# Spreading the reciprocals of the denominators through device memory instead of with matmuls

## The chip, the core and the metric

The kernel runs on one core of one Trainium2 chip. The metric is the device time of one execution in microseconds (us). Before the change the median of three runs is 1918.21 us (1917.11 to 1920.19).

## The reference, cut to what matters

The input is 16 sequences of 1024 tokens with 512 features (16384 tokens). The attention layer is a causal linear attention with 16 heads of 32 features, run over groups of sequences; its output is added to the input. A mixture of experts with a capacity follows. With these inputs no expert stays within its capacity, so the kernel's second part has nothing to do beyond the test for it.

```python
x_n = layernorm(x)
q = elu(x_n @ Wq.T + bq) + 1          # per head, 32 features
k = elu(x_n @ Wk.T + bk) + 1
v = x_n @ Wv.T + bv
# per head, over the tokens of a sequence, causal:
kv_t = kv_(t-1) + outer(k_t, v_t)
ks_t = ks_(t-1) + k_t
o_t  = (q_t . kv_t) / (q_t . ks_t + 1e-6)
x1 = x + o @ Wo.T + bo
```

The change concerns `1 / (q_t . ks_t + 1e-6)`, one number for each token and head. The kernel multiplies it into `q` before the scores and the state products, so every one of a head's 32 rows of `q` needs the head's reciprocal.

## The kernel before, in words

A block is 512 tokens (`BT`), four tiles of 128 (`TPB`); there are 32 blocks, two to a sequence. Features lie on the partitions in four groups of 128 (`KD`), each with four heads of 32 rows. All of it is one program of hand-ordered instruction streams, one for each engine, unrolled over steps. The step at offset `t` does the attention of block `t` ("attn"), the projections of block `t+1` ("proj") and the normalising of block `t+2` ("turn"). There is a step at -2 that only turns, one at -1 without attention, full steps 0 to 29, step 30 without turning, and step 31 with attention alone. A step has four stages, `c` = 0 to 3.

TensorE (PE) in a stage: first two chunks of projections (K and Q in stages 0 and 1, V in 2 and 3), then from the state (L771), the new state (L801), values within the tile (L788), the scores of the next tile (L758), two more chunks (L666 for K and Q, L684 for V), and the output projection O (L684). Results pass through a ring of six PSUM banks, `ring`, whose uses are listed in order by `ring_uses()`; each use waits until the use six places earlier was freed by the engine that reads it. `SKIPS` pads the list to a multiple of six.

The denominators take this way, all in stage 2 of the step that projects the block, with the divided `q` needed from stage 3 on:

- VectorE (DVE) sums the keys over the tokens with a scan into `k_sum` (L994), GpSimd (POOL) multiplies it by `q_raw` in place (L1315).
- PE sums each head's 32 rows (`denominators`, L730): 8 matmuls, each 256 columns wide, after the values within the tile. The two halves of the block's tokens lie on different rows.
- ScalarE (ACT) copies the bank to `den` and adds epsilon (L944), DVE takes the reciprocal of 128x256 (L1220). ACT and DVE split it in a rounded and a remaining part (L950, L1231).
- PE spreads the reciprocals to all rows of their heads (`spread_reciprocals`, L743): 8 matmuls with 32 rows of contraction, 256 columns wide, into four banks of the ring, at the end of stage 2, behind O.
- DVE multiplies the four banks by `q_raw` into `q_div` (`divide`, L1032), at the start of its stage 3.

DVE's order in stage 3 of a full step is: `divide`, the moments of the residual of tile 2 (L1091, L1094), values of chunk V2 (L1003, L1005), `split_x_low` of tiles 0 and 1 (L1048), a transpose of keys (L1022), `o_lo` (L1215), the state (L1072), four masks (L973), `split_x_low` of tile 2, values of V3, `split_x_low` of tile 3, and then the residual of tile 3 (L1084). PE begins the next step with the chunk K0 (L666), which reads all of `xt` and waits for all four `split_x_low`:

```python
elif c == 0:
    pe.wait_ge(xt_lo.handle, xt_lo.at(TPB * (st.off + 1)))
```

All DMAs are issued by the sync engine (SP) in one order. In stage 2: load of the residual of tile 3 (L578), `send_keys` of tile 3 to device memory (L556), `fetch_keys` back in another arrangement (L568, four DMAs, waiting for the send to land), and the store of tile 2 (L585). Moments of a block take a like way: 4 KB out (L544) and 512 KB back, the same row for all partitions (L547, `x_rows`). POOL in stage 2 normalises `x_in` with eight operations of 128x512 that read `x_in` and `x_rows` (L1308, L1310) and then adds the output's bias to the next residual (L1387).

## Time and profile before

| | us |
|---|---|
| median of three runs | 1918.21 |
| the profiled execution's own time | 1917.13 |
| span of its instructions | 1915.3 |
| PE busy | 1890.7 (99% of the span) |
| DVE busy | 1565.8 (82%) |
| POOL busy | 890.4 (46%) |
| ACT busy | 664.1 (35%) |
| DMA queue of the data | 214.13 MB, 35.0% of 16 engines |

Busy shares are means over the span. In the timeline a line has the start, the duration, the engine, the source line and the operation; brackets hold idle time of the engine before it and what ended it. Matmul durations overlap, so what a matmul costs is read from start to start. A duration with "x4" is that of four instructions merged. Start times below are from the span's start. A step takes some 58.5 us ((1858.4 - 44.8) / 31, from the first starts of L730 in the first and the last block).

### The profile page before, as it was taken

How to read it: one execution, taken by the hardware profiler on the slowest of the kernel's cores; microseconds unless marked ns; L12 is line 12 of the kernel's file. 1: busy time of each engine (PE TensorE's matmuls, PEld its weight loads, DVE VectorE, ACT ScalarE, POOL GpSimd, SP SyncE). 2: the span in 40 equal slices, each digit the busy share in tenths (PEclk: the TensorE clock that was granted, in tenths of full speed). 3: DMA queues.
4: the chain of work that ended last, by engine and by line, in shares of the span. 5: the costliest groups of instructions: out<-in, count | busy, mean ns of one | idle time of the engine just before them, and what ended most of it. 6: DMA issues, size and time to landing. Idle time of an engine off the chain costs nothing.

```text
span 1915.3 us, 60195 instructions
## 1 busy us (share of the span) xinstructions
PE 1890.7 (99%) x25412; PEld 1659.7 (87%) x25412; DVE 1565.8 (82%) x3356; ACT 664.1 (35%) x1298; POOL 890.4 (46%) x981
## 2 busy tenths in 40 slices
PE   7999999999999999999999999999999999999997
PEld 6888888888888888888888888888888888888886
DVE  7888787878879887878878887887788897878887
ACT  4333333333333333333333333333333333323331
POOL 4345544455453555534554435545345544355422
PEclk9999999999999999999999999999999999999999
DMA  6343334333233332343423334323443334343222
GB/s 215 101 128 111 99 103 128 117 123 115 85 124 122 123 123 75 122 126 112 126 95 109 117 118 136 111 83 116 125 126 112 98 104 129 116 128 118 78 68 90
DMA packets 171200, 218.00 MB, mean 114 GB/s; under 512 B 24369, under 2 KB 85809, under 8 KB 170929
## 3 DMA queue, kind: packets, MB, share of 16 engines
q1 hardware_dynamic: 170928, 214.13, 35.0%
q8 instruction: 201, 3.29, 0.7%
q14 instruction: 71, 0.57, 0.1%
HBM read 151.02 MB, written 63.04 MB: 112 GB/s over the span
## 4 chain that ended last, share of the span: by engine, by line
PE 97%; DVE 2%; POOL 1%; issue 0%; ACT 0%; POOLq 0%; DVEq 0%
PE ring L684 39%; PE ring L666 37%; PE ring L758 7%; PE num_ps L788 6%; PE num_ps L771 3%; PE num_ps L801 2%; PE ring L730 1%; PE ring L743 1%; DVE s_mask L973 0%; PE ring L654 0%; DVE stats L1091 0%; PE num_ps L378 0%; DVE res L1084 0%; DVE q_div L1032 0%; DVE xt_lo L1048 0%
## 5 line engine op out<-in xcount | busy, mean ns | idle before, releaser
L1315 POOL TENSOR_TENSOR k_sum<-k_sum,q_raw 128x512 f32<-128x512 f32 x128 | 165.3, 1291 | 545.7 <-DVE q_raw L984 545.7
L883 ACT ACTIVATE e_tmp<-ring,bias_n 128x512 f32<-128x512 f32 x256 | 176.2, 688 | 509.1 <-PE ring L666 508.5
L973 DVE TENSOR_TENSOR s_mask<-ring,causal 128x512 f32<-128x512 f32 x512 | 314.5, 674 | 0.0
L684 PE MATMUL ring<-wv_hi,xt_hi 128*128 128x260 f32 x1024 | 299.0, 292 | 0.0
L684 PE MATMUL ring<-wv_hi,xt_lo 128*128 128x260 f32 x1024 | 289.2, 282 | 0.0
L684 PE MATMUL ring<-wv_lo,xt_hi 128*128 128x260 f32 x1024 | 289.2, 282 | 0.0
L684 PE MATMUL ring<-wo_lo,o_hi 128*128 128x260 f32 x1016 | 285.7, 282 | 0.0
L684 PE MATMUL ring<-wo_hi,o_lo 128*128 128x260 f32 x1016 | 285.6, 284 | 0.0
L684 PE MATMUL ring<-wo_hi,o_hi 128*128 128x260 f32 x1016 | 284.8, 281 | 0.2 <-ACT o_hi L938 0.2
L938 ACT ACTIVATE o_hi<-num_ps 128x512 fp32r<-128x512 f32 x127 | 75.8, 597 | 464.7 <-PE num_ps L788 464.7
L666 PE MATMUL ring<-xt_hi,wk_hi 128*128 128x512 f32 x512 | 207.2, 405 | 3.1 <-DVE xt_lo L1042 1.7
L1310 POOL TENSOR_TENSOR x_in<-x_in,x_rows 128x512 f32<-128x512 f32 x124 | 203.9, 1644 | 9.7
L1308 POOL TENSOR_TENSOR x_in<-x_in,x_rows 128x512 f32<-128x512 f32 x124 | 198.2, 1598 | 18.1 <-DMA x_rows<-moments_rows 18.1
L684 PEld LDWEIGHTS ring<-wv_hi,xt_hi 128*128 128x128 f32 x1024 | 192.7, 188 | 12.1 <-issue 0.4
L666 PE MATMUL ring<-xt_hi,wk_lo 128*128 128x512 f32 x512 | 200.2, 391 | 0.0
L666 PE MATMUL ring<-xt_hi,wq_lo 128*128 128x512 f32 x512 | 199.6, 390 | 0.0
L666 PE MATMUL ring<-xt_lo,wk_hi 128*128 128x512 f32 x512 | 199.3, 389 | 0.0
L666 PE MATMUL ring<-xt_hi,wq_hi 128*128 128x512 f32 x512 | 199.2, 389 | 0.0
L666 PE MATMUL ring<-xt_lo,wq_hi 128*128 128x512 f32 x512 | 199.2, 389 | 0.0
L684 PEld LDWEIGHTS ring<-wo_hi,o_hi 128*128 128x128 f32 x1016 | 191.3, 188 | 3.0 <-ACT o_hi L938 0.4
L684 PEld LDWEIGHTS ring<-wv_hi,xt_lo 128*128 128x128 f32 x1024 | 193.2, 189 | 0.0
L684 PEld LDWEIGHTS ring<-wo_lo,o_hi 128*128 128x128 f32 x1016 | 190.6, 188 | 2.9
(147 smaller groups left out, 3948.2 us busy)
## 6 DMA issues: line engine op xcount, KB each, us to landing
x_tok<-in_x SPq DMA_DIRECT2D x128, 256.0 KB, 3.7
res<-in_x SPq DMA_DIRECT2D x128, 256.0 KB, 2.8
out<-res SPq DMA_DIRECT2D x128, 256.0 KB, 2.1
x_in<-in_x_t SPq DMA_DIRECT2D x124, 256.0 KB, 4.5
keys_turned<-k_turned SPq DMA_DIRECT2D x112, 256.0 KB, 2.0
k_tok<-keys_turned SPq DMA_DIRECT2D x448, 64.0 KB, 2.1
x_rows<-moments_rows SPq DMA_DIRECT2D x31, 512.0 KB, 3.6
k_t<-in_wk_t SPq DMA_DIRECT2D x4, 256.0 KB, 4.3
```

The costliest lines, as they stand in the source:

```text
L666: mm = pe.matmul(bank, w[a][:, k, g * P:(g + 1) * P], xt[b][:, k, :], start=n == 0, stop=n == 3 * KD - 1)
L684: mm = pe.matmul(bank[:, 0:HW], rows[a](k), w[b][:, k, h, :], start=n == 0, stop=n == 3 * KD - 1)
L758: mm = pe.matmul(ring[:, st.bank(u), g * P:(g + 1) * P], k_t[rows, par, g, t], q_div[rows, par, g, t], start=True, stop=True, skip_group_c ...
L771: pe.matmul(out, kv_diag[rows, g, j * HD:(j + 1) * HD], q_div[rows, st.off % 2, g, c * P:(c + 1) * P], start=g < 2, stop=False, skip_group ...
L788: mm = pe.matmul(out, v_tok[:, c, head:head + HD], s_mask[:, j, g], start=first_tile(st, c) and g < 2, stop=g >= 2, skip_group_check=True, ...
L801: pe.matmul(kv_ps[j * HD:(j + 1) * HD, g * HD:(g + 1) * HD], k_tok[:, n % 2, j, g], v_tok[:, c, cols], start=first_tile(st, c) and g == 0, ...
L883: act.activation(e_tmp[:, m], bank, ACT.Relu, bias=bias_n[:, m, g:g + 1], scale=-1.0).then_inc(phi_relu.handle, 1)
L938: act.activation(o_wide[0], num, ACT.Copy).then_inc(o_hi.handle, 1)
L973: dve.tensor_tensor(s_mask[:, j], ring[:, st.bank(u)].rearrange("p (g t) -> p g t", g=KD), repeat(causal, KD), ALU.mult).then_inc(free[st. ...
L1308: pool.tensor_tensor(x, x, repeat(x_rows[:, :, c, 0], KD), ALU.subtract).then_inc(x_centred.handle, 1)
L1310: pool.tensor_tensor(x, x, repeat(x_rows[:, :, c, 1], KD), ALU.mult).then_inc(x_normed.handle, 1)
L1315: pool.tensor_tensor(k_sum[:, g], k_sum[:, g], q_raw[:, g], ALU.mult).then_inc(prod.handle, 1)
```

## The change

The matmuls that spread the reciprocals go, with the split in two parts and the four ring banks. The denominators are laid out as 128 rows by 128 columns: a row is a head and a tile of tokens. `denominators` becomes 16 matmuls of 128 columns in place of 8 of 256, the outer loop over tiles, and moves ahead of the values within the tile (`from_tile`) on PE. ACT's copy to `den` moves ahead of `o_hi`, DVE's reciprocal ahead of `o_lo`. SP writes the 64 KB of reciprocals to device memory between `send_keys` and `fetch_keys` of tile 3, and behind `fetch_keys` reads them back with four DMAs, one for each head's place in its group, each to 32 partitions of `k_sum` (256 KB each, 1 MB in all). DVE divides in two instructions of 128x1024, both operands in SBUF, where before it were four of 128x512 with one operand in PSUM. PE's scores wait for the half that they read. The scratch space that a later choice shared with `den` becomes a tensor of its own.

```diff
-SKIPS = {0: 1, 3: 2}
+SKIPS = {3: 1}
...
-        uses += [("O", (c, 0)), ("O", (c, 1))] + [("R", g) for g in range(KD)] * (c == 2)
+        uses += [("O", (c, 0)), ("O", (c, 1))]
...
+        def send_reciprocals(b):
+            sp.wait_ge(den_rec.handle, b + 1)
+            sp.dma_start(den_dram.rearrange("g r t -> (g r) t"), den).then_inc(den_out.handle, 16)
+
+        def spread_reciprocals(b):
+            sp.wait_ge(den_out.handle, 16 * (b + 1))
+            for j in range(HPG):
+                rows = den_dram[:, j * TPB:(j + 1) * TPB, :].rearrange("g s t -> g (s t)").unsqueeze(0)
+                sp.dma_start(k_sum[j * HD:(j + 1) * HD], rows.to_broadcast([HD, KD, BT])).then_inc(den_in.handle, 16)
...
                 if c == 2:
                     send_keys(t, 3)
+                    if st.has("proj"):
+                        send_reciprocals(t + 1)
                     fetch_keys(t, 3)
+                    if st.has("proj"):
+                        spread_reciprocals(t + 1)
...
-            for g in range(KD):
-                for s in range(2):
-                    mm = pe.matmul(bank[g * HD:(g + 1) * HD, 0:BT // 2], head_cols[:, s],
-                                   k_sum[:, g, s * BT // 2:(s + 1) * BT // 2], start=s == 0, stop=s == 1,
-                                   tile_position=(0, g * HD))
+            for s in range(TPB):
+                for g in range(KD):
+                    mm = pe.matmul(bank[g * HD:(g + 1) * HD, 0:P], head_cols[:, s],
+                                   k_sum[:, g, s * P:(s + 1) * P], start=s == 0, stop=s == TPB - 1,
+                                   skip_group_check=True, tile_position=(0, g * HD))
...
-        def spread_reciprocals(st):
-
-            pe.wait_ge(rden_parts.handle, rden_parts.at(st.lin(1, st.off + 1, 1)))
...
+            if c % 2 == 0:
+                pe.wait_ge(divided.handle, 2 * off + c // 2 + 1)
...
                     add_state(st, c)
+                    if c == 2 and proj:
+                        denominators(st)
                     from_tile(st, c)
...
+        def invert(st):
+
+            dve.wait_ge(free[BANK[("DEN", 0)]].handle, st.freed(("DEN", 0)))
+            dve.reciprocal(den, den).then_inc(den_rec.handle, 1)
+
+        def divide(st, half):
+
+            dve.wait_ge(den_in.handle, 16 * HPG * (st.off + 2))
+            t = slice(half * BT // 2, (half + 1) * BT // 2)
+            dve.tensor_tensor(q_div[:, (st.off + 1) % 2, :, t], k_sum[:, :, t], q_raw[:, :, t], ALU.mult
+                              ).then_inc(divided.handle, 1)
...
                 if last and proj and attn:
-                    divide(st)
-                if last and attn and proj:
+                    divide(st, 0)
+                    divide(st, 1)
                     residual_moments(st, 2)
```

In step -1, which has no attention, the first half is divided after two `split_x_low`, the second after the values of V3.

## Rows read from the trace of the kernel before

**Rows 1.** The page, part 1: busy time and share of the span.
```profile
PE 1890.7 (99%) x25412; PEld 1659.7 (87%) x25412; DVE 1565.8 (82%) x3356; ACT 664.1 (35%) x1298; POOL 890.4 (46%) x981
```

**Rows 2.** The waits of PE: waiter, releaser, total us, times, longest.
```profile
PE ring L666 <- DVE xt_lo L1042: 1.7, 1, 1.7
```

**Rows 3.** Timeline of PE in step 15: start, duration, line, operation.
```profile
913.37 0.28 PE L684 MATMUL ring<-wo_hi,o_lo 128*128 128x260 f32 x1
913.49 0.28 PE L684 MATMUL ring<-wv_hi,xt_hi 128*128 128x260 f32 x1
...
917.32 1.10 PE L788 MATMUL num_ps<-s_mask,v_tok 128*32 128x128 f32 x32
918.20 1.10 PE L730 MATMUL ring<-k_sum,head_cols 128*32 128x256 f32 x16
919.23 1.17 PE L758 MATMUL ring<-q_div,k_t 32*128 32x128 f32 x32
...
926.07 0.28 PE L684 MATMUL ring<-wo_hi,o_lo 128*128 128x260 f32 x1
926.28 0.51 PE L743 MATMUL ring<-rden,spread 32*128 32x256 f32 x8
926.72 0.39 PE L684 MATMUL ring<-wv_hi,xt_hi 128*128 128x260 f32 x1
926.94 0.28 PE L684 MATMUL ring<-wv_lo,xt_hi 128*128 128x260 f32 x1
...
938.66 0.39 PE L666 MATMUL ring<-xt_hi,wk_hi 128*128 128x512 f32 x1
```

**Rows 4.** Timeline of DVE in the same step.
```profile
919.90 1.74 DVE L1220 RECIPROCAL den<-den 128x256 f32<-128x256 f32 x1
...
923.89 0.74 DVE L1231 SCALAR_TENSOR_TENSOR rden<-rden_high,lo_rows,den 128x256 fp32r<-128x256 f32 x1
...
926.82 2.48 DVE L1032 TENSOR_TENSOR q_div<-ring,q_raw 128x512 f32<-128x512 f32 x4
...
930.93 1.28 DVE L1048 TENSOR_TENSOR xt_lo<-x_in,xt_hi 128x512 fp32r<-128x512 f32 x2
932.13 0.70 DVE L1022 STREAM_TRANSPOSE k_turned<-k_t 128x512 f32<-128x512 f32 x1
...
937.32 0.67 DVE L1048 TENSOR_TENSOR xt_lo<-x_in,xt_hi 128x512 fp32r<-128x512 f32 x1
...
943.83 2.11 DVE L994 TENSOR_TENSOR_SCAN k_sum<-k_t 128x512 f32<-128x512 f32 x1
```

**Rows 5.** Timeline of POOL in the same step.
```profile
922.66 1.69 POOL L1308 TENSOR_TENSOR x_in<-x_in,x_rows 128x512 f32<-128x512 f32 x1
...
929.39 1.29 POOL L1387 TENSOR_TENSOR res<-res,bo_row 128x512 f32<-128x512 f32 x1
...
943.57 1.28 POOL L1387 TENSOR_TENSOR res<-res,bo_row 128x512 f32<-128x512 f32 x1
```

**Rows 6.** Timeline of SP in the same step: the fetch of keys of tile 3.
```profile
921.92 1.74 SPq L568 DMA_DIRECT2D k_tok<-keys_turned  x4
```

**Rows 7.** The DMA issues: count, KB each, median us from issue to landing.
```profile
x_rows<-moments_rows SPq DMA_DIRECT2D x31, 512.0 KB, 3.6
...
moments_rows<-mv SPq DMA_DIRECT2D x31, 4.0 KB, 1.4
```

**Rows 8.** The same three places in another step, from the timelines.
```profile
686.88 1.74 SPq L568 DMA_DIRECT2D k_tok<-keys_turned  x4
...
691.90 2.48 DVE L1032 TENSOR_TENSOR q_div<-ring,q_raw 128x512 f32<-128x512 f32 x4
...
694.20 1.29 POOL L1387 TENSOR_TENSOR res<-res,bo_row 128x512 f32<-128x512 f32 x1
```

**Rows 9.** Two windows with fetched keys: engines busy, then PE clock, DMA share, GB/s.
```profile
1768.30:1768.70 0.40, 0.40 (x16) 0.38 (x16) 0.40 (x2) 0.27 (x1) 0.00 (x0) 1.00 1.15 337
...
1769.00:1769.40 0.40, 0.40 (x20) 0.30 (x12) 0.36 (x2) 0.02 (x1) 0.24 (x1) 1.00 1.21 213
```

More of the change, by code:

```diff
@@ L416, in set_constants @@
         link(pool.memset(head_cols, 0.0))
-        for s in range(2):
-            for h in range(2):
-                row = 2 * HPG * s + HPG * h
-                link(pool.tensor_copy(head_cols[:, s, row:row + HPG], head_of_row))
+        for s in range(TPB):
+            rows = head_cols[:, s, 0:HPG * TPB].rearrange("p (j s) -> p j s", j=HPG)
+            link(pool.tensor_copy(rows[:, :, s], head_of_row))
         link(pool.memset(kv_diag, 0.0))
-        link(pool.memset(row_of_group, 0.0))
-        for g in range(KD):
-            link(pool.affine_select(out=row_of_group, in_=row_of_group, compare_op=ALU.not_equal, fill=1.0,
-                                    base=-g * HD, pattern=[[-1, 2 * 2 * HPG]], channel_multiplier=1))
         for e in range(E):
@@ L832, in body @@
                     sum_columns(pe)
-                if c == 2 and proj:
                     denominators(st)
@@ L838, in body @@
                     scores(st, st.off + 1, 0)
-                if last and not attn:
-                    spread_reciprocals(st)
                 if proj:
@@ L930, in body @@
                     exponential(act, 4)
+                if c == 2 and proj:
+                    u = ("DEN", 0)
+                    act.wait_ge(full[st.bank(u)].handle, st.filled(u))
+                    act.activation(den, ring[:, st.bank(u), 0:P], ACT.Copy, bias=DEN_EPS
+                                   ).then_inc(free[st.bank(u)].handle, 1)
                 if st.alone() and last:
@@ L1194, in body @@
                     chunks(st, c, 0, 1)
-                if last and not attn:
-                    divide(st)
                 if c == 0 and not attn:
@@ L1201, in body @@
                     split_x_low(st, 1)
+                if last and not attn:
+                    divide(st, 0)
                 if c == 2 and attn:
@@ L1207, in body @@
                     turn_keys(st.off, 2)
+                if c == 2 and proj:
+                    invert(st)
                 if st.alone() and last:
@@ L1246, in body @@
                 if last and not attn:
+                    divide(st, 1)
                     mask_scores(st, 0)
@@ L1271, in set_first @@
                 split_low(dve, name, g)
-            set_from_constants(dve)
+            for name in BY_COLUMNS:
+                dve.wait_ge(ready[name].handle, KD)
+            dve.wait_ge(const_set.handle, CONSTS)
             dve.wait_ge(row_load.handle, ROWS)
```

70 lines of the change are left out of this document (10 added, 60 removed).

## The prediction
> **What bounds the kernel now.** I read the page's busy times first: PE is busy 99% of the span and no other engine more than 82% [rows 1]. Then the waits of PE: in the steady steps it waits for nobody; the entry for `xt_lo` is a single wait at the start [rows 2]. So time is PE's instructions from start to start. The third view is DVE's timeline in stage 3, because the share of 82% hides what this stage looks like. There DVE runs without a gap from the divides at 926.82 to the last `xt_lo`, which ends at 937.32 + 0.67 = 937.99: 11.17 us in one piece [rows 4]. PE's next K0, which reads that `xt_lo`, starts at 938.66, 11.84 us after the divides' start [rows 3]. Slack there is only 0.67 us in a step of 58.5. The reader is to see two bounds nearly level: PE everywhere, and from stage 3 to the next step a DVE chain that begins with exactly the instruction that the change touches.
>
> **PE, what goes.** Around the spread the starts are 926.07 (last of O), 926.28 (spread), 926.72 and 926.94 (first and second of V2): 0.87 us for what takes two ordinary distances of 0.12 (913.37 to 913.49) where O is followed by V directly [rows 3]. So 0.87 - 0.24 = 0.63 us go per spread, the change of tiling on both sides included. 32 spreads: 20.2 us. If nothing else happened, the span would be 1915.3 - 20.2 = 1895.1.
>
> **PE, denominators.** As many columns as before (16 x 128 against 8 x 256). Values and denominators now take 917.32 to 919.23, 1.91 us together [rows 3]. The values' matmuls have just the new shape (128 rows, 32 columns of weights, 128 streamed) and take 0.88 until the next start. I take 0 for narrower and earlier denominators; ends -0.1 (four groups alternate sooner) and +0.9 (twice the values' time), the nearest row being that of the values.
>
> **ACT and DVE, stage 2.** The reciprocal has half the columns: 1.74 us becomes about 0.9; the combination of two parts (0.74) goes [rows 4]. Neither moves the divides: DVE waits ahead of them for O's last half from PE. `o_hi` and `o_lo` come up to 0.9 us later behind the denominators, but PE needs `o_lo` only after a V chunk of about 3 us (24 distances of 0.12 [rows 3]): 0. If that cover were gone, it would cost 0.9 a step.
>
> **SP and the transfer.** The old reciprocal ended at 919.90 + 1.74 = 921.64 [rows 4]; the new one ends about two microseconds sooner, before the fetch of keys is issued at 921.92 [rows 6], which waits for the keys' own way out. So the send fits in at no cost. The fetch issues for 1.74 us, and only then, at 923.66, the spread begins to be issued; nothing else on SP is urgent (the store of tile 2 comes near 927). The trace has no DMA of this kind. The nearest row is the spread of the moments, also one row read for many partitions: 512 KB land in 3.6 us, where 4 KB land in 1.4 [rows 7]. That is 2.2 us for 512 KB, 4.4 for 1 MB, 5.8 with the fixed part: landing at 923.66 + 5.8 = 929.46, 2.64 us after the time at which DVE now starts dividing. In the other step: 686.88 + 1.74 + 5.8 = 694.42, 2.52 after 691.90 [rows 8]. Bounds of the landing: at 337 GB/s, the faster window, 1 MB takes 3.1 + 1.4 = 4.5; at 150 GB/s (a third under the slower window's 213 [rows 9]) 7.0 + 1.4 = 8.4; and if the four overlap wholly, the last, issued 1.3 us after the first, might land 2.6 later, 3.9 in all. Offsets E from the old start of the divides are then 1.3, 5.1 and 0.7.
>
> On this the Trainium skill has a rule (SBUF — State Buffer, Door 1: The DMA port swizzle): a transfer that covers only 32 partitions reaches half of the ports, with 189 GB/s given for 1 MiB, about 5.5 us by that figure. The trace agrees only in part: keys, also 32 partitions a DMA, reach 337 GB/s in one window and 213 in the next [rows 9]. The sum would hardly differ by it, but it speaks against the quick landing.
>
> **The divides.** From SBUF 1024 columns cost about 1.2 us (two `xt_lo` from 930.93 to 932.13 [rows 4]); two divides 2.3 to 2.4, against 2.4: I take 0.1 less. But now both operands are in SBUF. The old combination, with its operands in SBUF, started at 923.89 while POOL's operation ran until 922.66 + 1.69 = 924.35, and it took 0.74 us, to 924.63: just 256 columns' time after POOL's end. The scan at 943.83 ran beside POOL's 943.57 to 944.85 and took 2.11 for 512 columns [rows 4, 5]. DVE stood until POOL was through. The divide meets this: POOL's L1387 starts at 929.39 (and 694.20, 2.30 after the old divides), lasts 1.29, and the reciprocals land at about its start [rows 5, 8]. The first divide then effectively starts at POOL's end, 3.59 after the old divides in one step and 3.86 in the other. I take E = 3.6. An earlier landing changes little: POOL is busy with such operations all the way before, and each divide can meet one. Ends of the clash: 0 and 1.3 (one operation) behind a landing.
>
> The skill states the same as a rule (SBUF — State Buffer, Who interferes with whom): a VectorE instruction with two inputs in SBUF excludes a GpSimd one that reads SBUF, for the whole instruction. The two rows above agree with it.
>
> **The sum.** Next K0 is ready at E + 11.17 - 0.1 after the old divides, and was at 11.84: a step grows by E - 0.77, down to the floor of -0.63. With 3.6 this is +2.83 us. Waits of PE at the scores (first divide done at 3.6 + 1.2) and for V2's banks fall into the same delay and are not added. Steps 0 to 29 have the `xt_lo` chain: 30 x 2.83 = 84.9. Steps -1 and 30 lack it or have other cover, each between -0.63 and +2.8; I take 0.7 each, 1.4. Span 1915.3 + 84.9 + 1.4 = 2001.6; outside the span the profiled execution has 1917.13 - 1915.3 = 1.8, so 2003.4. It was 1.1 us under the median of 1918.21; I predict 2003.
>
> **Rivals.**
> (a) Late transfer without the clash: E = 2.6, +1.83 a step, 54.9 in all, 1974. For it: only two rows show the clash, and the landing may fall behind POOL's operation or ahead of it. Against it: POOL has no gap there. With the quicker 4.5 us and no clash, E = 1.3, +0.53, 1935.
> (b) A slower transfer: from E = 3.9 on the landing decides alone, and at 5.1 a step grows by 4.33: 130, 2050. For it: the 213 GB/s window. Against: the moments' row.
> (c) Faster: the transfer is hidden. It wins if the divides start less than 0.77 us later than now, clash included, and gives the whole 0.63 a step from E = 0.14 down: 1895.1 + 1.8 = 1897; at E = 0.5, 1909. For it: DMA engines are mostly idle in stage 2, and four queued DMAs overlap. Against: 1 MB must land 3.9 us after its first issue, when half of it takes 3.6 [rows 7], and POOL must let both divides through.
> (d) The change doesn't save on PE: narrow denominators cost 0.9 more. Under a DVE-bound step part of that is on the path too: up to 2003 + 28 = 2031.
>
> **Chances.** Forecast (1990 to 2015) 0.50; (a) 0.22, of which 0.05 under 1940; (b) 0.12; (c) 0.09, and between (c) and (a), level with now, 0.04; (d) 0.03. The range is 1938 to 2028: it leaves out (c), the level case and some of (a)'s low end, about 0.15, and the upper part of (b) and (d), about 0.06. What a measurement can tell from no change is 0.2%, about 4 us: faster 0.09, same 0.04, slower 0.87.
>
> **What would show it.** In the changed profile PE gets waits that it lacked: K0 (`xt_hi`, `wk_hi`) for DVE's `xt_lo`, some 2 us a step, and smaller ones at scores and V3. DVE's `q_div` shows idle time of about 2.5 us ended by the DMA into `k_sum`, and the first divide takes over 2 us instead of 1.2 if it meets POOL. The four DMAs into `k_sum` show their first issue behind the keys' fetch and a landing of 4 to 5 us each. L684 follows L684 at 0.12 at the end of stage 2. I am wrong if DVE doesn't idle before `q_div`, if the last `k_sum` DMA lands within 4 us of the first issue, or if K0 doesn't wait.

## The result and the profile after

| | before | after |
|---|---|---|
| median of the runs shown together | 1918.41 us (6 runs, 1917.11 to 1920.67) | 2048.59 us (6 runs, 2046.87 to 2052.86) |
| the profiled execution: time, span | 1917.13, 1915.3 | 2052.3, 2050.3 |
| TensorE clock granted over the span | 0.998 | 0.971 |

The ratio is 1.068, with a 95% interval of 1.0669 to 1.0691: the kernel became 130 us slower. The forecast was 85 us slower, 2003 us, and its range ended at 2028. The direction was right, the size was not.

Part 1 of the page after stands against [rows 1]. DVE has less to do (1543.3 us against 1565.8) and is busy for a smaller share of a longer span; PE is no longer busy all the time.

```profile
PE 1925.7 (94%) x25668; PEld 1703.2 (83%) x25668; DVE 1543.3 (75%) x3257; ACT 649.4 (32%) x1266; POOL 895.6 (44%) x976
```

PE's waits after (waiter, releaser, total us, times, longest), against [rows 2]:

```profile
PE ring L679 <- DVE gate_x L979: 44.6, 31, 2.3
PE ring L740 <- DVE q_div L1009: 44.3, 25, 4.3
...
PE ring L661 <- DVE xt_lo L1026: 4.7, 8, 0.6
```

L679 `<- gate_x` is chunk V3 waiting for a bank that DVE empties late; L740 are the scores, which need the divided `q`; L661 is K0, and PE stands there for `xt_lo` in only 8 of the steps. The cause behind them is DVE's own wait at the divides, once in each of the 32 steps:

```profile
DVE q_div L1009 <- DMA k_sum<-den_rows: 117.2, 32, 7.2
```

The DMA issues after (count, KB each, median us to landing), against [rows 7]:

```profile
k_sum<-den_rows SPq DMA_DIRECT2D x128, 256.0 KB, 5.0
...
den_rows<-den SPq DMA_DIRECT2D x32, 64.0 KB, 2.0
```

**A step with a fetch of keys.** SP's timeline, with the send of keys, the send of reciprocals, the fetch [rows 6], the spread and the store of tile 2:

```profile
984.29 1.17 SPq L535 DMA_DIRECT2D keys_turned<-k_turned  x1
985.52 0.42 SPq L552 DMA_DIRECT2D den_rows<-den  x1
987.45 1.74 SPq L547 DMA_DIRECT2D k_tok<-keys_turned  x4
989.24 1.86 SPq L558 DMA_DIRECT2D k_sum<-den_rows  x4
992.36 0.36 SPq L574 DMA_DIRECT2D out<-res  x1
```

DVE's timeline of the same step, against [rows 4]:

```profile
992.11 0.15 DVE L1063 TENSOR_TENSOR gate_o<-ring,g_bo 128x4 f32<-128x4 f32 x1
996.80 2.78 DVE L1009 TENSOR_TENSOR q_div<-k_sum,q_raw 128x1024 f32<-128x1024 f32 x2 [4.54 <-DMA k_sum<-den_rows]
...
1007.59 0.68 DVE L1026 TENSOR_TENSOR xt_lo<-x_in,xt_hi 128x512 fp32r<-128x512 f32 x1
```

DVE is free at 992.26. The last of the four DMAs has landed at 996.80, 7.56 us after the first issue at 989.24. From there DVE's chain runs as it did before: it ends at 1008.27, and K0 starts 0.06 behind it. PE, against [rows 3]:

```profile
995.40 1.10 PE L770 MATMUL num_ps<-s_mask,v_tok 128*32 128x128 f32 x32
998.59 1.17 PE L740 MATMUL ring<-q_div,k_t 32*128 32x128 f32 x32 [2.09 <-DVE q_div L1009]
1000.94 0.59 PE L679 MATMUL ring<-wv_hi,xt_hi 128*128 128x260 f32 x1 [1.18 <-DVE gate_x L979]
1001.33 0.42 PE L679 MATMUL ring<-wv_lo,xt_hi 128*128 128x260 f32 x1
1001.54 0.42 PE L679 MATMUL ring<-wv_hi,xt_lo 128*128 128x260 f32 x1
...
1008.33 0.50 PE L661 MATMUL ring<-xt_hi,wk_hi 128*128 128x512 f32 x1
```

After its two waits PE starts V3's matmuls 0.21 us apart (1001.33 to 1001.54), where 0.12 was the distance. Windows of 3 us show why (columns as in [rows 9]: the fourth and third numbers from the end are POOL's instruction count and PE's granted clock, then DMA share and GB/s):

```profile
990.00:993.00 3.00, 3.00 (x27) 3.00 (x26) 0.99 (x4) 0.43 (x1) 2.92 (x3) 1.00 0.82 218
993.00:996.00 3.00, 3.00 (x101) 2.67 (x103) 0.00 (x0) 0.00 (x0) 2.92 (x2) 1.00 1.02 223
...
1002.00:1005.00 3.00, 3.00 (x18) 3.00 (x18) 3.00 (x6) 1.01 (x4) 0.00 (x0) 0.61 0.36 135
```

Two things are to be seen. While the reciprocals come in, all 16 DMA engines are busy (share 1.02), yet all traffic together is only 223 GB/s. And after PE's waits its clock is granted at 0.61 on average in 1002 to 1005: at the lower of its two levels, 1.2 GHz (0.50), until past 1004, and at 2.4 GHz behind it.

**A step without a fetch.** Only every second block sends its fourth tile of keys through device memory, so in every second step the spread follows its own send directly. SP, DVE and POOL in such a step:

```profile
1048.75 0.32 SPq L552 DMA_DIRECT2D den_rows<-den  x1
1050.29 2.03 SPq L558 DMA_DIRECT2D k_sum<-den_rows  x4
```

```profile
1057.57 3.86 DVE L1009 TENSOR_TENSOR q_div<-k_sum,q_raw 128x1024 f32<-128x1024 f32 x2 [1.69 <-DMA k_sum<-den_rows]
```

```profile
1056.44 1.69 POOL L1286 TENSOR_TENSOR x_in<-x_in,x_rows 128x512 f32<-128x512 f32 x1
1058.09 2.26 POOL L1363 TENSOR_TENSOR res<-res,bo_row 128x512 f32<-128x512 f32 x1
```

The landing comes earlier here (DVE is free at 1055.88 and waits 1.69 us), and so it meets POOL: the two divides take 3.86 us instead of 2.36, and POOL's L1363 takes 2.26 instead of 1.25.

**All steps.** T0 is the time at which DVE is free for the divides, E the divides' start behind it, K0 the first matmul of the next step. Means of steps 0 to 28 (29 steps) of the two timelines, in us:

```
                          T0->K0   E     both divides   then to end of last xt_lo   K0->next T0
before, with a fetch      11.84   0.00      2.48              8.69                     47.35
before, without           11.54   0.00      2.48              8.51                     46.73
after,  with a fetch      16.35   4.89      2.31              8.79                     47.51
after,  without           14.84   2.46      3.48              8.57                     46.87
```

A step thus grew by 4.51 + 0.16 = 4.67 us with a fetch and by 3.30 + 0.14 = 3.44 without, 4.06 on average. In terms: 3.68 of later start (mean E), 0.42 of longer divides (5.79 / 2 against 2.48), 0.08 in the rest of DVE's chain; less 0.61, the mean slack that K0 had behind that chain before; plus 0.34 by which PE now ends behind DVE's chain, and 0.15 between K0 and the next T0. The sum is 4.06. Over the whole span, T0 of step 0 comes 9.0 us later (step -1 waits for its reciprocals too: PE stands 3.4 us for `q_div` and 3.4 us for the masks there), the 30 steps from there add 123.7 and the end 2.3: 135.0 = 2050.3 - 1915.3.

### The profile page after: what moved, and what is told of

The parts are those of the page before. It is cut to its first block, busy times and chain, and to the rows that moved or that the text cites. A ratio compares the mean times of both kernels' runs of the same rounds, so it can differ in the third digit from the quotient of the medians.

```text
span 2050.3 us, 60660 instructions
## 1 busy us (share of the span) xinstructions
PE 1925.7 (94%) x25668; PEld 1703.2 (83%) x25668; DVE 1543.3 (75%) x3257; ACT 649.4 (32%) x1266; POOL 895.6 (44%) x976
## 4 chain that ended last, share of the span: by engine, by line
PE 66%; DMA 15%; DVE 13%; SPq 4%; issue 1%; ACT 0%; POOL 0%; DVEq 0%; POOLq 0%
PE ring L661 35%; PE ring L679 21%; DMA k_sum<-den_rows 9%; DVE q_div L1009 5%; PE ring L740 3%; DMA keys_turned<-k_turned 3%; PE num_ps L770 3%; SPq L558 2%; PE num_ps L753 2%; SPq L547 2%; DMA den_rows<-den 2%; DVE s_mask L947 1%; PE num_ps L783 1%; DVE v_tok L977 1%; DVE stats L1069 1%
## 5 line engine op out<-in xcount | busy, mean ns | idle before, releaser
L679 PE MATMUL ring<-wv_hi,xt_hi 128*128 128x260 f32 x1024 | 313.9, 307 | 44.6 <-DVE gate_x L979 44.6
L679 PE MATMUL ring<-wv_hi,xt_lo 128*128 128x260 f32 x1024 | 307.9, 301 | 0.0
L679 PE MATMUL ring<-wv_lo,xt_hi 128*128 128x260 f32 x1024 | 306.8, 300 | 0.0
L679 PE MATMUL ring<-wo_hi,o_hi 128*128 128x260 f32 x1016 | 286.2, 282 | 3.5 <-DVE s_mask L947 3.3
L679 PE MATMUL ring<-wo_lo,o_hi 128*128 128x260 f32 x1016 | 286.4, 283 | 0.0
L679 PE MATMUL ring<-wo_hi,o_lo 128*128 128x260 f32 x1016 | 285.6, 284 | 0.4 <-DVE o_lo L1195 0.4
L679 PEld LDWEIGHTS ring<-wv_hi,xt_hi 128*128 128x128 f32 x1024 | 211.5, 206 | 54.8 <-DVE gate_x L979 50.8
L661 PE MATMUL ring<-xt_hi,wk_hi 128*128 128x512 f32 x512 | 210.6, 411 | 10.0 <-DVE xt_lo L1026 4.7
L679 PEld LDWEIGHTS ring<-wv_lo,xt_hi 128*128 128x128 f32 x1024 | 211.7, 207 | 0.0
L679 PEld LDWEIGHTS ring<-wv_hi,xt_lo 128*128 128x128 f32 x1024 | 211.3, 206 | 0.0
L1284 POOL TENSOR_TENSOR x_in<-x_in,x_rows 128x512 f32<-128x512 f32 x124 | 198.7, 1603 | 25.5 <-DMA x_rows<-moments_rows 25.5
L883 ACT ACTIVATE kv_diag<-kv_sum 32x128 f32<-32x128 f32 x448 | 138.0, 308 | 215.1 <-DVE kv_sum L1050 184.6
L1286 POOL TENSOR_TENSOR x_in<-x_in,x_rows 128x512 f32<-128x512 f32 x124 | 199.1, 1606 | 9.7
L661 PE MATMUL ring<-xt_hi,wk_lo 128*128 128x512 f32 x512 | 201.6, 394 | 0.0
L661 PE MATMUL ring<-xt_lo,wk_hi 128*128 128x512 f32 x512 | 200.7, 392 | 0.0
L661 PE MATMUL ring<-xt_hi,wq_lo 128*128 128x512 f32 x512 | 199.6, 390 | 0.0
L679 PEld LDWEIGHTS ring<-wo_hi,o_hi 128*128 128x128 f32 x1016 | 192.8, 190 | 7.8 <-issue 4.7
L661 PE MATMUL ring<-xt_hi,wq_hi 128*128 128x512 f32 x512 | 199.2, 389 | 0.0
L661 PE MATMUL ring<-xt_lo,wq_hi 128*128 128x512 f32 x512 | 199.2, 389 | 0.0
```

The source lines that it names most:

```text
L661: mm = pe.matmul(bank, w[a][:, k, g * P:(g + 1) * P], xt[b][:, k, :], start=n == 0, stop=n == 3 * KD - 1)
L679: mm = pe.matmul(bank[:, 0:HW], rows[a](k), w[b][:, k, h, :], start=n == 0, stop=n == 3 * KD - 1)
L883: act.activation(kv_diag[rows, :, rows], kv_sum[rows], ACT.Copy).then_inc(kv_kept.handle, 1)
L1284: pool.tensor_tensor(x, x, repeat(x_rows[:, :, c, 0], KD), ALU.subtract).then_inc(x_centred.handle, 1)
L1286: pool.tensor_tensor(x, x, repeat(x_rows[:, :, c, 1], KD), ALU.mult).then_inc(x_normed.handle, 1)
```

## Experiments

Three kernels of this section (those without a spread, with half of it, and the kernel before with divides from `k_sum`) work with wrong quotients, with which the second part of the kernel, the experts, has work to do; their whole times say nothing, and only the steps of the attention part are read. Two more (all rows, and another source) also have wrong quotients, but in them the second part has nothing to do, as their times of 2075 and 2039 us show. "Step" is the distance of the reciprocals' starts, 58.49 us before and 62.71 after.

### Is it the landing or the clash?

The changed kernel without the spread's DMAs; the divides wait for the send alone.

```diff
         def spread_reciprocals(b):
-            for j in range(HPG):
-                sp.dma_start(k_sum[j * HD:(j + 1) * HD], rows.to_broadcast([HD, KD, BT])) ...
         def divide(st, half):
-            dve.wait_ge(den_in.handle, 16 * HPG * (st.off + 2))
+            dve.wait_ge(den_out.handle, 16 * (st.off + 2))
```

> Left out: the four DMAs that bring the reciprocals back; the divides multiply by what lies in k_sum and wait only for the send of the reciprocals, so the output is not the reference's. All other parts of the change stay. Theory A (the transfer's lateness is the whole loss): PE is the bound again and has 0.63 us a step less, about 1898. Theory B (the divides from SBUF are also stopped by GpSimd's operations, which run without a gap at that time): DVE's chain to the next K0 grows by 0.9 to 2 us against a slack of 0.04, 1921 to 1958, and the first divides take over 1.5 us in the trace.

Measured: 60.12 us a step, 1.63 over before, with no landing to wait for. Both divides together take 4.33 us in one step. So 2.6 of 4.2 us go with the transfer, and 1.6 remain. The two don't add up to shares of landing and clash: without the transfer every divide meets POOL, with it most of them come later.

The kernel before, with one operand of the divides taken from SBUF (L1032 reads `k_sum` instead of the bank); no transfer.

```diff
-                dve.tensor_tensor(q_div[:, ..., g], bank, q_raw[:, g], ALU.mult)
+                dve.tensor_tensor(q_div[:, ..., g], k_sum[:, g], q_raw[:, g], ALU.mult)
```

> The kernel before with one edit: its four divides read k_sum in SBUF in place of the PSUM bank (which they still free), so the quotient is wrong and nothing else moves. Theory A (two operands in SBUF are stopped by GpSimd): each divide of 0.6 us can wait for one operation of GpSimd, 1 to 4 us more in the chain of DVE, 1930 to 2020. Theory B (no clash for this operation): 1918, the divides at 0.68 us each.

Measured: 61.25 us a step, 2.76 over before. DVE's and POOL's timelines show it plainly:

```profile
970.44 5.44 DVE L1032 TENSOR_TENSOR q_div<-k_sum,q_raw 128x512 f32<-128x512 f32 x4
```

```profile
969.41 1.60 POOL L1308 TENSOR_TENSOR x_in<-x_in,x_rows 128x512 f32<-128x512 f32 x1
971.09 1.96 POOL L1310 TENSOR_TENSOR x_in<-x_in,x_rows 128x512 f32<-128x512 f32 x1
972.98 1.75 POOL L1387 TENSOR_TENSOR res<-res,bo_row 128x512 f32<-128x512 f32 x1
```

Four divides of 0.62 us each take 5.44 us beside three operations of POOL, and POOL's last two are longer too: 1.96 and 1.75 us, where the kernel before has 1.66 and 1.29 (the 1.29 is in [rows 5]):

```profile
927.79 1.66 POOL L1310 TENSOR_TENSOR x_in<-x_in,x_rows 128x512 f32<-128x512 f32 x1
```

The clash is real and worth 2.8 us a step, if the divides start when POOL is busy. In the changed kernel they start later, beside POOL's last one or two operations or behind them.

The converse: the kernel before with a transfer of the same size and place (the source is the input, since the matmul spread stays), and with its divides, which still read PSUM, waiting for it. A second version has the transfer, and nobody in stage 3 waits for it.

```diff
+        def spread_rows(b):
+            sp.wait_ge(den_rec.handle, b + 1)
+            for j in range(HPG):
+                sp.dma_start(k_sum[j * HD:(j + 1) * HD], <8 KB of x>.to_broadcast([HD, KD, BT])).then_inc(den_in.handle, 16)
         def divide(st):
+            dve.wait_ge(den_in.handle, 16 * HPG * (st.off + 2))     # in the first version only
```

> The kernel before, with a transfer like the changed kernel's (four DMAs of 256 KB, one 8 KB run of the input x read for 32 partitions each, into k_sum, issued behind the third fetch of keys) and with the divides waiting for it too; they still read their factor from PSUM, so the result is the reference's and no divide has both operands in SBUF. Theory A, the late landing is the larger part of the loss: the last DMA lands 7 to 8 us after the first issue, 4 to 5 us after the old start of the divides, and the step of 58.49 us grows by 3.5 to 4.2 to about 62.4, 2030 to 2050 us, as slow as the changed kernel though it has no clash. Theory B, the clash of DVE with POOL is the larger part: the step grows by 1.9 or less, up to 1978 us. The theories are told apart at about 2005 us.

> The same transfer beside the kernel before, awaited by nobody in stage 3 (only the next writer of k_sum, some 20 us later, waits for it). Theory A, traffic costs nothing by itself, only waiting for it does: within 5 us of before, 1915 to 1925 us. Rival, the 1 MB takes bandwidth that other transfers of stage 3 or the engines' access to SBUF need: 0.5 us a step or more, 1936 us or above, with the loss in waits for k_tok, res or in longer POOL and DVE operations.

Measured: awaited 1994.81 us (1992.07 to 2000.76), ratio 1.0396 [1.0375, 1.0417]; beside 1921.49 us (1918.04 to 1924.08), ratio 1.0004 [0.9994, 1.0014]. PE's waits in the awaited version:

```profile
PE ring L768 <- DVE q_div L1043: 23.9, 16, 3.9
PE ring L676 <- DVE xt_lo L1059: 15.8, 27, 0.6
PE ring L694 <- DVE s_mask L983: 10.0, 24, 0.6
```

1 MB more a step costs nothing by itself; waiting for it costs 75 us with no clash. Theory A expected 2030 or more, theory B at most 1978: the value lies between. The awaited landing is 7.02 us after the first issue here, and as there is no send in front of it the first issue is earlier: E is 3.50 with a fetch and 1.74 without, 2.62 on average. Less the slack of 0.61 this is 2.0, and the step grew by 2.38. K0 waits for `xt_lo` in 27 steps: here DVE's chain sets the step, as the prediction had it (the remaining 0.4 of the growth isn't broken down). The changed kernel's mean E is 1.06 larger, and its step 1.84 longer.

### What holds the landing back?

Three forms of the transfer: four DMAs over all 128 partitions (one row of `den_rows` each, so with a wrong row for most heads); two of the four DMAs; and another source, in which each partition reads 8 KB of its own of the input, in place of one row for all.

```diff
-            for j in range(HPG):
-                sp.dma_start(k_sum[j * HD:(j + 1) * HD], rows.to_broadcast([HD, KD, BT])) ...
+            for g in range(KD):                                                    # all rows
+                sp.dma_start(k_sum[:, g], rows.to_broadcast([P, BT])) ...
+            for j in range(HPG // 2):                                              # half
+                sp.dma_start(k_sum[j * HD:(j + 1) * HD], <8 KB of x for each partition>) ...   # other source, all j
```

> The same 1 MB in four DMAs of 128 runs of 2 KB, still one row read for many, but each DMA to all 128 partitions of one group of k_sum; three quarters of the rows get another head's reciprocals. Theory A (a DMA to 32 partitions goes at about half rate, 200 to 240 GB/s as the trace after shows): data in 2.7 to 3 us instead of 5, the divides start some 2 us sooner, 1960 to 2005. Theory B (many reads of one row, or the queue, set the rate): the rate stays and the time stays at 2045 to 2052.

> Left out: the reciprocals of the two upper heads of each group (two of the four DMAs, 512 KB). Theory A (bytes at the low rate set the landing): 2.4 us of data less and 0.9 us of issuing less, 1960 to 2005. Theory B (fixed latency and the place in the queue set it): under 1 us a step, 2020 to 2045.

> The changed kernel with other source rows for the four DMAs: each partition reads its own 8 KB of the input instead of all reading the same rows of 64 KB of reciprocals; the quotient is wrong, so only the attention part's steps are read. Destination, sizes and order are the same: 32 partitions each. Theory A (32 partitions set the rate): landing and rate as in the changed kernel, 200 to 240 GB/s, 62.7 us a step. Theory C (many reads of the same rows of device memory set it, which would explain that DMAs to all rows were no faster): 350 to 400 GB/s, the last lands about 5.5 us after the first issue instead of 7.6, and a step takes 60.5 to 61.5 us.

The issues of the three, in that order (median us from a DMA's issue to its landing in the last column):

```profile
k_sum<-den_rows SPq DMA_DIRECT2D x128, 256.0 KB, 5.6
```

```profile
k_sum<-den_rows SPq DMA_DIRECT2D x64, 256.0 KB, 4.4
```

```profile
k_sum<-in_x SPq DMA_DIRECT2D x128, 256.0 KB, 4.7
```

Measured: all rows 2074.76 us (2070.06 to 2077.69), ratio 1.0801 [1.0779, 1.0823]; landing 8.3 us after the first issue (median of 32), against 7.5; the time is above both theories' ranges. Half: 60.98 us a step, which is theory A's, bytes. The other source: 2038.56 us (one time), landing 7.1 us after the first issue, where theory C expected 5.5. So it is neither the reach over 32 partitions nor the one row that all read. Nor is it the length of the runs: the awaited and the other-source version read 8 KB at a time, the changed kernel 2 KB, and they land at 7.0, 7.1 and 7.5. The Trainium skill (SBUF — State Buffer, Door 1: The DMA port swizzle) would have the 128-partition form faster; here it was slower, and the measurement decides.

The landings of the single DMAs tell more than the rate. From the first issue on, the changed kernel's four land at 3.77, 5.00, 6.25 and 7.43 us, and the two of the half version at 3.76 and 5.06 (medians of 32): each 256 KB adds 1.2 us, and the first alone takes 3.8. The kernel before has transfers of this form too. It loads `x_tok` and `x_in` with four DMAs of 256 KB each, and the last of them lands 6.4 us (`x_tok`, median of 32) and 6.9 us (`x_in`, of 31) after the first issue. In its page they are (median us of a single DMA, where the spread has 5.0):

```profile
x_tok<-in_x SPq DMA_DIRECT2D x128, 256.0 KB, 3.7
x_in<-in_x_t SPq DMA_DIRECT2D x124, 256.0 KB, 4.5
```

The changed kernel with the store of tile 2 held back until the spread has landed, and with the spread issued ahead of the fetch of keys:

```diff
+                if c == 2 and st.has("proj"):                        # store held back
+                    sp.wait_ge(den_in.handle, 16 * HPG * (t + 2))
                 if st.has("proj") or last:
                     store(st, c)
```

```diff
                         send_reciprocals(t + 1)                      # spread first
+                        spread_reciprocals(t + 1)
                     fetch_keys(t, 3)
-                    if st.has("proj"):
-                        spread_reciprocals(t + 1)
```

> The changed kernel, with the store of tile 2 (256 KB, until now issued some 3 us after the first of the four spread DMAs) issued only when these have landed. Theory A, the DMA engines move about 225 GB/s in this stretch whoever asks, and the store is served among the spread: the landing comes 256 KB / 225 GB/s = 1.1 us sooner, a step falls from 62.71 to about 61.6, some 2014 us (2005 to 2025). Theory B, the spread is limited by something of its own and the store takes nothing from it: 2049 within 5. Theory C, the store now delays res for the next tile: slower than 2055.

> The changed kernel, with the spread issued ahead of the third fetch of keys, nothing else moved. Theory A, E (the landing behind the old start of the divides) falls by the fetch's 1.8 us of issue, from 4.6 to 2.8, and a step falls by 1.5 to 1.8: 1991 to 2002 us, if the keys are not missed. Theory B, the keys then land behind the spread's 1 MB and the matmuls on num_ps wait for k_tok up to 3 us, in half of the steps, as they did in the version that also divides late: 2005 to 2035 us. Theory C, engines are shared so that the order of issue changes nothing: 2049 within 5.

Measured: store held back 2049.69 us (2045.35 to 2052.69), 1.0664 [1.0644, 1.0683], landing 7.4 us after the first issue: the store takes nothing from the spread. Spread first 2022.14 us (2019.97 to 2025.43), 1.0533 [1.0516, 1.0551]: theory B. E falls to 3.04 in the steps with a fetch, and the keys come late instead (theirs is the second line):

```profile
PE ring L678 <- DVE gate_x L978: 36.0, 29, 2.3
PE num_ps L782 <- DMA k_tok<-keys_turned: 17.3, 15, 2.6
```

In all forms that move the whole 1 MB the landing is 7.0 to 8.3 us after the first issue (medians). It isn't peculiar to `k_sum` or to this stage, since the loads of `x_tok` and `x_in` take nearly as long; `x_tok`'s four land at 2.9, 4.0, 5.2 and 6.4 us. What makes the spread's first DMA land only at 3.8 us, and what holds the rate near 220 GB/s behind it, stays open.

### Is the DVE chain the path, or PE's waits and its clock?

The changed kernel with the divides behind the moments, V2's values, two `xt_lo` and the transpose:

```diff
                 if last and proj and attn:
-                    divide(st, 0)
-                    divide(st, 1)
                     residual_moments(st, 2)
...
                     turn_keys(st.off + 1, 0)
+                    divide(st, 0)
+                    divide(st, 1)
```

> Only DVE's order in stage 3 changes: the moments of tile 2, values V2, two x_lo splits and the keys' transpose come ahead of the two divides, which follow where they would meet the landed reciprocals. Theory A (the step is set by DVE's chain behind the late divides): some 4 us of that chain move into the idle time, a step takes 59 to 60.5 us instead of 62.7, 1935 to 1980; PE still waits some 1.5 us at the scores. Theory B (the step is set by PE's own waits at the scores and by its slower clock after them): the scores wait as before, little changes, 2020 to 2050.

Measured: 2046.23 us (2040.0 to 2048.68), 1.0653 [1.063, 1.0675], although DVE no longer idles. PE's longest entry:

```profile
PE ring L740 <- DVE q_div L1009: 88.2, 32, 4.1
```

The wait moved from DVE to PE and cost the same. The forecast's sum, in which PE's waits at the scores fall into the delay of DVE's chain, is not the whole story.

The changed kernel with eight matmuls of 512 columns that nobody reads, put ahead of the scores' wait in stage 3:

```diff
+            if c == 0 and off:
+                for n in range(8):
+                    pe.matmul(ring[:, st.bank(scores_of(c)[0])], w_q[0][:, 0, 0:P], w_k[0][:, 0], ...)
             if c % 2 == 0:
                 pe.wait_ge(divided.handle, 2 * off + c // 2 + 1)
```

> The changed kernel with eight matmuls of 512 columns more a step, whose results are overwritten, put ahead of PE's wait for the divided q in stage 3. They fill some 1.8 us in which PE stands. Theory A (the step ends on DVE's chain, PE's half clock lies beside it): the granted clock goes up, the time stays at 2040 to 2055. Theory B (the half clock is on the path): 1 to 1.7 us a step come back, 1995 to 2018.

Measured: 2036.76 us (2035.9 to 2041.61), 1.0616 [1.0599, 1.0634], between the two theories. More work made the kernel 12 us faster than the changed one. The clock over the span is 0.992 instead of 0.971, and now K0 waits for DVE:

```profile
PE ring L661 <- DVE xt_lo L1030: 15.9, 27, 0.6
PE ring L679 <- DVE gate_x L983: 14.4, 16, 1.6
```

The lower clock after PE's stalls was on the path for 12 / 31 = 0.4 us a step; DVE's chain is the next bound, right behind it. T0 to K0 is 16.04 and 14.51 here, 0.31 and 0.33 less than after: 0.10 of it is a smaller E, and 0.23 is K0's lag behind DVE's chain, which falls from 0.34 to 0.11. That is two thirds of the term of 0.34 in the sum above.

### Can the landing be covered?

First the spread ahead of the fetch, one divide behind V2's values and the other at the end of the step:

```diff
                     chunks(st, c, 0, 1)
+                if last and proj and attn:
+                    divide(st, 0)
...
                         residual_moments(st, c)
+                if last and proj and attn:
+                    divide(st, 1)
```

> SP issues the reciprocals' spread ahead of the fetch of keys; DVE divides the first half behind values V2 and the second half at the end of the step. Theory A: the landing comes 1.7 us sooner, the first divide is ready about when PE wants the scores, and the second has left the chain: 58 to 59.5 us a step, 1900 to 1950. Theory B (the fetched keys, now behind 1 MB, stop PE at the new state instead): 60 to 62 us a step, 1960 to 2020, with waits of PE on the keys in the trace.

Measured: 1953.51 us (1950.85 to 1955.29), 1.0178 [1.0161, 1.0195], just behind theory A's range; the waits on the keys are theory B's.

```profile
PE ring L739 <- DVE q_div L1008: 17.9, 16, 3.5
PE num_ps L782 <- DMA k_tok<-keys_turned: 17.6, 16, 3.0
```

Then, with the transfer as it is, the consumers moved: PE computes the scores of the next block behind V3 instead of ahead of it (about 3 us later; `ring_uses` follows), DVE divides behind `o_lo` and the state (first version) or ahead of them (second), and masks last.

```diff
-                if last and proj and attn:
-                    scores(st, st.off + 1, 0)
                 if proj:
                     chunks(st, c, 2, 3)
-                if last and not attn:
+                if last and proj:
                     scores(st, st.off + 1, 0)
```

> The changed kernel with the transfer as it is, but its consumers moved out of its way: PE computes the scores of the next block's first tile after the last chunk of values instead of ahead of it (some 3 us later; the ring's list of uses follows), and DVE divides both halves after the residual's moments, the third tile's values, two xt_lo, a transpose, o_lo and the state's sum, and masks the scores after the last xt_lo. Theory A, the loss is only that the divides and scores wait for a landing 2.5 us (steps without a fetch of keys) to 4.9 us (steps with one) behind DVE's old start: with the consumers some 4 to 8 us later nothing waits, the removed PE work shows, and the step is 58.73 - 0.63 = 58.1 or a little above, 1897 to 1915 us. Rival B, the clash of the divides with POOL or DVE's later mask takes PE's waits elsewhere (s_mask, o_lo, K0): 1925 to 1960 us. Rival C, the transfer costs something even where nobody waits: above 1960 us.

> The same, with the divides ahead of o_lo and the state's sum. Theory A: the divides stand some 4.5 us after DVE's old start, so that steps without a fetch of keys have no wait and those with one a wait of DVE under 1 us, which PE may see at o_lo: 1897 to 1925 us, not faster than the other order. Rival, the divides' place decides and the later one makes the scores wait (q_div on PE): then this one is faster than the other by over 5 us.

Measured: 1965.74 us (1963.85 to 1967.69), 1.0238 [1.0224, 1.0252]; and 2023.86 us (2019.17 to 2031.19), 1.0553 [1.0533, 1.0572], in which PE waits 31 times, 75.3 us, for V's banks. In the first the number is rival C's (above 1960), but not its mechanism: the landing is waited for only 4 times (3.5 us in all), and the time is in new waits of PE, as rival B had them. In the second the landing is waited for 5 times (4.9 us). PE's waits in the first:

```profile
PE ring L683 <- DVE gate_x L981: 30.9, 31, 2.4
PE ring L744 <- DVE q_div L1011: 16.0, 19, 3.6
```

Three further versions, each built on the one before it, move one DVE operation each: V3's values ahead of the third `xt_lo`; the second `xt_lo` behind the values too; and the first `xt_lo` ahead of V2's values, where DVE idles 0.94 us.

```diff
+                if proj and (attn or c != 2):          # 1: values ahead of xt_lo(2)
+                    chunks(st, c, 2, 3)
                 if last and turns:
-                    split_x_low(st, 0)                 # 3: to ahead of chunks(st, c, 0, 1)
-                    split_x_low(st, 1)                 # 2: to ahead of split_x_low(st, 2)
```

> The version with the scores after the values (1966 us; PE waits there 31 times for V3's bank, 30.9 us in all, and 19 times for q_div, 16.0 us), with DVE's copy of the fourth tile's values moved ahead of the third xt_lo, 0.68 us sooner. Theory A, what is left of the loss is only PE waiting for single DVE operations of this stage: 31 x 0.68 = 21 us less, 1945 us (1938 to 1952). Rival, PE meets the next wait at once (q_div, K0) or the cost is the transfer's own: 1955 us or more.

> The same, and the second xt_lo also behind the divides and the values, so that these start 0.65 to 1.3 us sooner. Theory A: both remaining waits of PE (for V3's bank and for q_div) shrink by another 0.7 us where the transfer has landed, 1920 to 1938 us, level with the kernel before or a little behind, since the steps with a fetch of keys wait for the landing again. Rival B: the landing decides (4.9 us behind the old start, in every second step) and the time stays that of the other version within 5 us; rival C: everything fits and the removed matmuls show, under 1912 us.

> The version with one xt_lo ahead of the divides (1941.5 us; 59.1 us a step), with that xt_lo moved ahead of the third tile's values, where DVE idles 0.94 us in each step between the two copies of values. Theory A, what is left is DVE's chain from stage 3 to the next K0 (31 waits for s_mask, 13.0 us) and single waits for values and q_div (11.5 us): the chain is 0.6 us shorter, and 31 x 0.42 of K0's waits and part of the others go, 1922 to 1930 us, level with the kernel before at best. Rival, this xt_lo meets POOL's normalising and takes over 1.2 us, so that nothing is gained: 1938 us or more.

Measured, in that order: 1944.83 us (1941.66 to 1947.78), 1.0127 [1.0108, 1.0145]; 1941.53 us (1939.57 to 1944.08), 1.0115 [1.0098, 1.0132]; 1940.79 us (1937.38 to 1946.37), 1.0109 [1.0093, 1.0125]. The first took back the 21 us that were expected of it, the wait for V3's bank falling from 30.9 to 13.2 us. The second is 3 us lower, which lies within the noise (the intervals overlap), and is rival B's number: the waits for `gate_x` and `q_div` fell, and K0 waits instead, for the masks:

```profile
PE ring L665 <- DVE s_mask L949: 13.0, 31, 3.0
...
PE ring L683 <- DVE gate_x L981: 6.0, 19, 2.0
```

The third gained nothing. The moved `xt_lo` meets POOL and takes 1.39 us instead of 0.68 in one step, 927 ns on average over all against 829:

```profile
L1028 DVE TENSOR_TENSOR xt_lo<-x_in,xt_hi 128x512 fp32r<-128x512 f32 x124 | 109.9, 927 | 0.0
```

None of the versions beats the kernel before. With the best, 108 of the 130 us are back though the transfer is the same. Some 22 us behind before, and about 42 behind what the removed matmuls would allow, are left; PE's remaining waits there (12.0 for the masks, 6.7 for `gate_x`, 6.4 for `q_div`) account for 25 of them, and the rest isn't settled.

## Why the prediction was right or wrong

**PE, what goes** and **denominators**: right. V2 follows O at 0.12 us:

```profile
991.45 0.28 PE L679 MATMUL ring<-wo_hi,o_lo 128*128 128x260 f32 x1
991.57 0.28 PE L679 MATMUL ring<-wv_hi,xt_hi 128*128 128x260 f32 x1
```

Denominators and values, in their new order, end 1.91 us after the first of them began (982.70 to 984.61), just what they took before, so the term of 0 holds, and rival (d) is out:

```profile
982.70 1.10 PE L725 MATMUL ring<-k_sum,head_cols 128*32 128x128 f32 x32
983.58 1.10 PE L770 MATMUL num_ps<-s_mask,v_tok 128*32 128x128 f32 x32
984.61 0.84 PE L740 MATMUL ring<-q_div,k_t 32*128 32x128 f32 x20
```

The 20.2 us can't be seen in the time, since another chain sets it.

**SP and the transfer**: this is the step that failed. The prediction took the spread's landing as 5.8 us after the first issue, from the moments' 3.6 us for half the bytes [rows 7]; it is 7.46 (median of 32; 7.25 to 8.77). Its upper bound, 150 GB/s, gave 8.4 and held the value; the value taken did not. The rate is the smaller part of the miss. The last three DMAs land 3.66 us behind the first, where the moments' row gives 3.3 for their bytes; the first lands at 3.77, where it gives 1.4 + 1.1 = 2.5. So 1.3 of the missing 1.7 us are in the first DMA, and the rate of the slower window [rows 9] with the same 1.4 us would have given only 6.3. The moments are one DMA of 512 KB, and "the trace has no DMA of this kind" was wrong in what mattered: `x_tok` and `x_in` are 1 MB in four DMAs of 256 KB, with landings of 6.4 and 6.9 us. The row of 213 GB/s, read as the keys' slower window, was mostly not keys: of its packets 38 of 512 bytes are theirs, 24 of 2 KB are the load of `x_in`, issued at 1767.45. The other half of this step was wrong too, in the other direction: it had the spread behind a fetch in every step. Both steps read for it ([rows 6] and [rows 8]) are ones with a fetch; every second has none, and there E is 2.46 instead of 4.89. In the steps with one, the first issue lies 2.8 us ahead of T0 on average, where 3.16 was taken; in those without, 5.0. The mean E is 3.68. That this is so near the 3.6 of the forecast is luck: the forecast had a quick landing behind a fetch, and a clash, in every step; measured are a slow landing in every step and no fetch ahead of it in half of them. The two errors nearly cancel.

**The divides**: the clash is shown, by the kernel before with divides from `k_sum`, in the form read off two rows. Its place was wrong. It was to decide in every step at E = 3.6. With a fetch the reciprocals land when POOL is nearly through, and the two divides take 2.31 us; without, they land early and take 3.48. It costs 0.42 a step on average, and a forecast with the measured landings and no clash would have missed by only that much.

**The sum.** A step grew by 4.06 and not by 2.83. The difference of 1.23 is: 0.60 from landing and clash together (3.68 + 0.42 against 3.6 - 0.1), 0.49 from what was "not added" (0.34 by which PE ends behind DVE's chain, 0.15 after K0), 0.08 in the rest of DVE's chain, and 0.06 from a slack of 0.61 in place of 0.67. The 0.49 is the second failure: PE's waits at the scores and at V3 don't fall wholly into DVE's delay, since a PE that has waited runs on at half its clock for some 3 us, in some steps 7. The filled version shows that this part is real, for 0.23 of it; where the 0.15 comes from isn't shown. The last 10 us are at the two ends: step -1 costs 9.0 us more and the end 2.3, where 0.7 was taken for each. Of the 9.0, 6.8 are PE's waits for the first `q_div` and for the masks behind it; the rest isn't broken down.

**The rivals.** The outcome is that of (b), in which the landing decides alone, with 4.33 a step and 2050 us. It holds for the steps with a fetch (E of 4.89, no clash); in the others the forecast's own mechanism, landing and then POOL, is at work. (b)'s 4.33 for every step is 0.27 above the mean of 4.06, and what the two ends cost makes up for it, so its 2050 is partly luck too. (b) was given 0.12 by the window of 213 GB/s against the moments' row; the range left its upper part out.

**What would show it.** Idle time at `q_div`, DMAs of 4 to 5 us each and the distance of 0.12 came as said (3.66 us of idle time instead of 2.5, and 5.0 us). K0's waits for `xt_lo`, some 2 us a step, did not: 4.7 us in all, while scores and V3 have 88.9. PE stood earlier, so that little was left to wait for at K0. DVE's chain still set K0 in 15 of the 29 steps of the table, where K0 starts 0.05 or 0.06 us behind the last `xt_lo`; in the other 14 PE comes 0.2 to 1.3 us later by itself.

## What to carry to other kernels

Moving work from a full engine to a DMA pays only if the first consumer already comes later than the slowest plausible landing; price that landing from a transfer of the same size in the same number of DMAs (here it was in the trace), not from a smaller one's median, and look at steps of every kind before multiplying one. When a full TensorE is made to wait, add to the wait what it runs on at the lower clock. To win the cover back, move the consumers rather than the transfer, and check that no one else on the same engine is then late.

## What the runs showed of the hardware

- 1 MB into `k_sum` in four DMAs of 256 KB landed 7.0 to 8.3 us after the first issue (medians), 3.8 us for the first DMA and 1.2 for each further one in the changed kernel; all traffic together was 218 to 223 GB/s meanwhile, with a DMA share of 0.82 to 1.02. 32 partitions or 128 a DMA, one row for all or a row each, runs of 2 or 8 KB made at most 1.2 us of difference, and four DMAs over 128 partitions were the slowest. In the kernel before, `x_tok` and `x_in` took 6.4 and 6.9 us in the same form, and one DMA of 512 KB 3.6 us.
- DVE and POOL exclude each other when both read SBUF with two operands, and both lose: divides of 0.68 us took 1.44 on average, and POOL's addition of 1.29 us took 2.26 in one step. The Trainium skill states the exclusion (SBUF — State Buffer, Who interferes with whom), and the trace agrees.
- Two waits of PE within 6 us (2.09 and 1.18) were followed by matmuls 0.21 us apart instead of 0.12, and by a granted clock of 0.61 over 3 us. Adding eight matmuls in front of the wait brought the clock over the span from 0.971 to 0.992 and made the kernel 12 us faster. The kernel before with divides from SBUF had waits of up to 1.8 us in the same place (33.7 us in 28, from 100 to 1800 us) and a mean granted clock of 1.00 there, with a single fall to the lower level, for 3.4 us.
